# Cross attention: output projection and residual once per pair of batches

## The reference, cut

```python
x = x + attn(layernorm(x), ...)
x = x + xattn(layernorm(x), ctx_1024, ...)     # the part that is changed
x = x + ffn(layernorm(x), ...)

def xattn(query, value, wq, bq, wk, bk, wv, bv, wo, bo):   # 16 heads of 8
    q = split_heads(query @ wq.T + bq); k = split_heads(value @ wk.T + bk); v = split_heads(value @ wv.T + bv)
    attn = softmax(einsum('bhqd,bhkd->bhqk', q, k) / sqrt(8))
    ctx = einsum('bhqk,bhkd->bhqd', attn, v)
    return merge_heads(ctx) @ wo.T + bo
```

## Time and profile before

| what | before |
|---|---|
| median of 3 runs | 630.91 us (628.44 to 633.17) |
| the profiled execution | 632.53 us, its span 630.3 us |
| mean granted TensorE clock | 0.978 |
| PE / PEld / DVE / ACT / POOL busy | 584.3 / 465.9 / 460.3 / 380.1 / 215.7 us |
| instructions | 17326 |

### The profile page before, as it was taken

The page is one execution under the profiler, slowest core; times in us unless marked ns, Lnnn a source line. Parts: engine busy times, 40 slices in busy tenths (PEclk is TensorE's granted clock), DMA queues, the critical chain, the costliest instruction groups (busy, mean ns, idle before and its releaser), DMA issues.

```text
span 630.3 us, 17326 instructions
## 1 busy us (share of the span) xinstructions
PE 584.3 (93%) x6542; PEld 465.9 (74%) x6542; DVE 460.3 (73%) x850; ACT 380.1 (60%) x602; POOL 215.7 (34%) x185
## 2 busy tenths in 40 slices
PE   3699787798999999999999999999999989999997
PEld 1566464476778778778777787877888768999985
DVE  4865456866887887887887887887787467676676
ACT  2457455265665665665665665665656676667762
POOL 4575324722242242242232232232221224433430
PEclk9889899799999999999999999999999999999999
DMA  5000005499266366366366366367380101211000
GB/s 219 1 3 3 0 2 119 86 192 210 77 148 147 99 146 151 93 146 156 88 146 162 88 141 166 88 137 172 79 197 3 51 1 60 73 62 57 1 0 34
DMA packets 25286, 59.91 MB, mean 95 GB/s; under 512 B 14104, under 2 KB 14488, under 8 KB 25248
## 3 DMA queue, kind: packets, MB, share of 16 engines
q1 hardware_dynamic: 25248, 59.38, 39.5%
HBM read 20.49 MB, written 0.52 MB: 33 GB/s over the span
## 4 chain that ended last, share of the span: by engine, by line
PE 68%; SPq 7%; ACT 3%; issue 3%; DVE 2%; DMA 1%; ACTq 0%; DVEq 0%
PE PS L1739 12%; PE PS L1723 12%; PE PS L1699 11%; PE PS L1869 6%; PE PS L225 6%; PE PS L1871 6%; PE PS L1870 5%; PE PS L217 5%; SPq L1080 3%; SPq L1073 3%; PE PS L1755 3%; ACT k_full L246 1%; SPq L1088 1%; DMA q_stack<-neg_rows 1%; PE PS L1709 1%
## 5 line engine op out<-in xcount | busy, mean ns | idle before, releaser
L1427 DVE TENSOR_REDUCE chunk_max<-PS 128x1 f32<-128x500 f32 x336 | 214.3, 673 | 60.8 <-PE PS L1699 59.2
L1268 ACT ACTIVATE P<-PS 125x896 f32<-125x896 f32 x192 | 173.5, 914 | 122.0 <-PE PS L1723 121.1
L1699 PE MATMUL PS<-k_hi,q_block_hi 128*128 128x500 f32 x336 | 131.2, 439 | 6.3 <-ACT k_full L246 3.3
L1723 PE MATMUL PS<-q_stack,k_stack 97*125 97x224 f32 x768 | 122.7, 283 | 3.3 <-DMA q_stack<-neg_rows 2.0
L1723 PEld LDWEIGHTS PS<-q_stack,k_stack 97*125 97x125 f32 x768 | 107.0, 190 | 18.2 <-issue 8.0
L255 POOL TENSOR_TENSOR k_lo<-k_full,k_hi 128x500 fp32r<-128x500 f32 x48 | 61.2, 1278 | 103.6 <-ACT k_full L246 101.3
L1699 PEld LDWEIGHTS PS<-k_hi,q_block_hi 128*128 128x128 f32 x336 | 61.0, 193 | 36.8 <-ACT k_full L246 16.7
L1739 PE MATMUL PS<-P,values 125*32 125x112 f32 x3072 | 83.6, 260 | 0.5 <-ACT P L1268 0.5
L1739 PEld LDWEIGHTS PS<-P,values 125*32 125x32 f32 x3072 | 72.0, 110 | 13.9 <-issue 10.7
L1161 POOL TENSOR_TENSOR q_stack<-q_copies,consts 96x896 fp32r<-96x896 f32 x16 | 26.9, 1678 | 132.0 <-PE PS L1723 131.6
L1592 DVE TENSOR_TENSOR PS<-gated,PS 128x448 f32<-128x448 f32 x64 | 40.2, 628 | 30.5 <-PE PS L1871 28.6
(11 more groups left out here) (192 smaller groups left out, 892.8 us busy)
## 6 DMA issues: line engine op xcount, KB each, us to landing
k_stack<-k_hi SPq DMA_DIRECT2D x128, 187.5 KB, 4.5
ctxT<-ctx_in SPq DMA_DIRECT2D x16, 750.0 KB, 4.4
k_stack<-k_lo SPq DMA_DIRECT2D x64, 187.5 KB, 4.5
w_gate_up<-wgu_in SPq DMA_DIRECT2D x8, 512.0 KB, 3.6
w_down<-wd_in SPq DMA_DIRECT2D x8, 256.0 KB, 3.7
q_stack<-neg_rows SPq DMA_DIRECT2D x112, 0.5 KB
mats<-mats_in SPq DMA_DIRECT2D x1, 832.0 KB, 5.6
q_copies<-q_hi SPq DMA_DIRECT2D x8, 98.0 KB, 4.6
```

What stands on the lines that cost most here:

```text
L1268: nc.scalar.activation(P[:, t % RING, :].rearrange("p (a n) -> p a n", a=2), PS[0:KR, 2 * (t % 2):2 * (t % 2) + 2, 0:HALF], ACT.Exp).then_ ...
L1427: nc.vector.tensor_reduce(out=chunk_max[:, n // KC, n % KC:n % KC + 1], in_=PS[:, max_bank(b, n), 0:KW], axis=AX.X, op=ALU.max).then_inc(m ...
L1699: nc.tensor.matmul(PS[:, max_bank(b, n), 0:KW], q_block_hi[:, j, 128 * t:128 * t + 128], k_hi[:, j, KW * c:KW * c + KW], start=True, stop= ...
L1723: last = nc.tensor.matmul(PS[0:KR, 2 * (t % 2) + g // 2, o:o + GH * N], k_stack[:, j, g, KR * t:KR * t + KR], q_stack[0:SHIFT_ROW + 1, j, ...
```

## The change

The projection and the residual are no longer done for each batch in the period behind it. They are done for both batches of a pair in slot 8 of the even period that follows, and for the last pair at the end. For this `heads_out2` has four parts of 2 x 64 columns, each batch's heads in its half, with the columns 56 to 63 of each half cleared once by POOL. The reciprocals have a tile of their own, `heads_inverse`. A projection loads all 128 columns of a part, and the residual adds 128 partitions. The counts of the semaphores follow the pairs. Before it writes the first half of a pair, `scale_heads` waits for the projection of the pair before.

Apart from this, the six matrices of the first stage move from `mats` into `mats1`, a tile of the first stage's memory, which stage two's tiles take over later. So there are two transfers for the weights in place of one, and the waits are for 48.

```diff
-                    sp.dma_start(mats[:, :, :], mats_in).then_inc(weights_loaded, 16)
+                    sp.dma_start(mats1[:, :, :], mats_in[:, 0:S1_MATS, :]).then_inc(weights_loaded, 16)
+                    sp.dma_start(mats[:, :, :], mats_in[:, S1_MATS:, :]).then_inc(weights_loaded, 16)
...
-            heads_out2 = sb2("heads_out2", [128, 4 * N])
+            heads_inverse = sb2("heads_inverse", [128, 4 * N])
+            heads_out2 = sb2("heads_out2", [128, 4, 2, PITCH])
...
                     pool.wait_ge(ones_ready, 1)
+                    nc.gpsimd.memset(heads_out2[:, :, :, N:PITCH], 0.0).then_inc(pads_cleared, 1)
+                    pool.wait_ge(pads_cleared, 1)
                     layernorm_power(pool, 4, slice(1, PAIRS))
...
-                        nc.vector.reciprocal(heads_out2[:, half], DEN[:, half]).then_inc(den_inverted, 1)
-
-                    def scale_heads(b):
+                        nc.vector.reciprocal(heads_inverse[:, half], DEN[:, half]).then_inc(den_inverted, 1)
+
+                    def scale_heads(b, j, u):
                         dve.wait_ge(den_inverted, 2 * b + 2)
-                        nc.vector.tensor_tensor(heads_out2[:, :], heads_out2[:, :], heads_sum[:, :], ALU.mult
-                                                ).then_inc(o_scaled, 1)
-
-                    def residual(b, j, u):
-                        dve.wait_ge(out_done, b + 1)
-                        r = slice(PITCH * j, PITCH * j + N)
-                        nc.vector.tensor_tensor(X[r, bass.ds(u, 1), :], X[r, bass.ds(u, 1), :],
-                                                OUT2[r, :].unsqueeze(1), ALU.add).then_inc(x2_ready, 1)
+                        if j == 0 and later(b, 2):
+                            dve.wait_ge(out_done, u)
+                        if isinstance(b, int) and b < 2:
+                            dve.wait_ge(pads_cleared, 1)
+                        by_part = [t[:, :].rearrange("p (a n) -> p a n", n=N) for t in (heads_inverse, heads_sum)]
+                        nc.vector.tensor_tensor(heads_out2[:, :, j, 0:N], *by_part, ALU.mult).then_inc(o_scaled, 1)
+
+                    def residual(u):
+                        dve.wait_ge(out_done, u + 1)
+                        nc.vector.tensor_tensor(X[:, bass.ds(u, 1), :], X[:, bass.ds(u, 1), :],
+                                                OUT2.unsqueeze(1), ALU.add).then_inc(x2_ready, 1)
...
-                                if t == OUT_SLOT:
-                                    residual(b - 1, 1 - j, u if j == 1 else u - 1)
+                                if t == OUT_SLOT and j == 0:
+                                    residual(u - 1)
...
-                    def project_out(b, j):
-                        pe.wait_ge(o_scaled, b + 2)
-                        take_bank(BANK_OF["out", 0], (x2_ready, b + 1))
+                    def project_out(u):
+                        pe.wait_ge(o_scaled, 2 * u + 3)
+                        take_bank(BANK_OF["out", 0], (x2_ready, u + 1))
                         for n in range(4):
-                            last = nc.tensor.matmul(OUT2[PITCH * j:PITCH * j + N, :], heads_out2[:, N * n:N * n + N],
+                            last = nc.tensor.matmul(OUT2, heads_out2[:, n, :, :].rearrange("p e n -> p (e n)"),
                                                     MAT[f"wo{n}"], start=(n == 0), stop=(n == 3))
                         last.then_inc(out_done, 1)
...
-                                if t == OUT_SLOT:
-                                    project_out(b - 1, 1 - j)
+                                if t == OUT_SLOT and j == 0:
+                                    project_out(u - 1)
...
                     for k in range(1, IT):
                         gates(0, 0, k)
-                    project_out(B - 1, 1)
+                    project_out(PAIRS - 1)
```

More of the change, by code:

```diff
@@ L40 @@
 MATS = ["Wqk_t", "Wv_t", "Wo_t", "Wqk_c", "Wv_c", "Wo_c", "wq", "wk", "wv", "wo0", "wo1", "wo2", "wo3"]
+S1_MATS = 6
 ROWS = ["gamma1", "gamma2", "bv", "bo"]
@@ L95, in build @@
         X = sb("X", [128, PAIRS, D])
-        mats = sb("mats", [128, len(MATS), D])
+        mats = sb("mats", [128, len(MATS) - S1_MATS, D])
         rows = sb("rows", [128, len(ROWS), D])
@@ L100, in build @@
         consts = sb("consts", [128, consts_in.shape[1]])
-        MAT = {n: mats[:, k, :] for k, n in enumerate(MATS)}
+        MAT = {n: mats[:, k, :] for k, n in enumerate(MATS[S1_MATS:])}
         ROW = {n: rows[:, k, :] for k, n in enumerate(ROWS)}
@@ L281, in build @@
         with s1:
+            mats1 = sb1("mats1", [128, S1_MATS, D])
+            MAT.update({n: mats1[:, k, :] for k, n in enumerate(MATS[:S1_MATS])})
             Z = sb1("Z", [128, PAIRS, D])
@@ L582, in _ @@
                     shift(1, 1)
-                    dve.wait_ge(weights_loaded, 32)
+                    dve.wait_ge(weights_loaded, 48)
                     nc.vector.tensor_tensor(wo_scaled[:, 0, :], MAT["Wo_t"], ROW["gamma1"], ALU.mult
@@ L669, in _ @@
                     turn_tokens(0)
-                    pe.wait_ge(weights_loaded, 32)
+                    pe.wait_ge(weights_loaded, 48)
                     for c in range(2):
@@ L1049, in build @@
             x2_ready = sem("x2_ready")
+            pads_cleared = sem("pads_cleared")
             TURN_REST, PROJECT_REST = 8, 12
@@ L1566, in period @@
                                 if t == SCALE_SLOT:
-                                    scale_heads(b - 1)
-                                if t == OUT_SLOT:
-                                    residual(b - 1, 1 - j, u if j == 1 else u - 1)
+                                    scale_heads(b - 1, 1 - j, u if j == 1 else u - 1)
+                                if t == OUT_SLOT and j == 0:
+                                    residual(u - 1)
                             if exists(mb, B):
@@ L1573, in period @@
                             if isinstance(b, int) and b == B - 2 and t == OUT_SLOT:
-                                dve.wait_ge(x2_ready, B - 2)
+                                dve.wait_ge(x2_ready, PAIRS - 1)
                                 norm_stats(range(PAIRS - 1))
@@ L1584, in _ @@
                         invert(B - 1, a)
-                    scale_heads(B - 1)
-                    residual(B - 1, 1, PAIRS - 1)
+                    scale_heads(B - 1, 1, PAIRS - 1)
+                    residual(PAIRS - 1)
                     def multiply(e, j, k):
@@ L1597, in split_hidden @@
                                                 ALU.subtract).then_inc(hidden_split, 1)
-                    dve.wait_ge(x2_ready, B)
+                    dve.wait_ge(x2_ready, PAIRS)
                     norm_stats(range(PAIRS - 1, PAIRS))
```

## The result

The changed kernel takes 625.62 us (median of 12 runs), the kernel before 630.94 us in the same comparison. The ratio is 0.9907, with a 95% interval of 0.9882 to 0.9932: 5.9 us less, between 4.3 and 7.4; the two medians by themselves differ by 5.3 us. Forecast were 626.2 us and 4.7 us. In a second comparison the ratio was 0.990 (0.9855 to 0.9945). In the comparisons of the experiments, three runs of the kernel before and one of a variant took 814 to 1835 us, and the ratios leave them out (the medians count them).

The account below looks back on a forecast made before the run. PE was taken to bound the kernel, busy 23.21 of 23.45 us a period in stage two. Removed projections save 5.5 us, wide loads lose 0.8: 630.9 - 4.7 = 626.2 us, range 622.0 to 630.0.

Parts of the forecast that it names:

- the larger term: Stage two, eight of sixteen projections removed: 5.5 us saved, 4.7 in odd periods 1 to 13 and 0.76 in period 15.
- the smaller term: The eight remaining projections load 128 columns instead of 56: 0.1 us lost each, 0.8 us in all.
- What bounds the kernel: Stage two: PE bounds it, busy 23.21 of 23.45 us a period; a projection costs the path 1.02 us.
- The odd periods lose 0.67 and not 1.01 us each: Slot 8, periods 1 to 13: waits for DVE leave 0.67 of the projection's 1.01 us, 4.7 us for seven periods.
- The two waits forecast: Odd periods: the turn waits for DVE's read of the values, slot 9's first maximum for DVE's reduction of maximum 0; 0.05 us latency.
- The last period: Period 15: the tile's scores after the removed projection wait for slot 7's exponentials and load 0.76 us earlier.
- The wide loads: Eight remaining projections: only the first load, behind its wait, is in the open; 0.8 us lost, between 0 and 3.8.
- What costs nothing: Residual, product with gaps, new wait in `scale_heads`, POOL's clearing, extra DMA at the start, and tail: each taken as 0.
- the whole projection is saved: Rival: DVE is less close behind PE, so eight projections save 8.2 us in all, 622.7 us; chance 0.2.
- Wide loads in the open: Rival: the 128-column loads of eight projections are exposed, 3.8 us lost, gain 1.7 us, 629.2 us; chance 0.13.
- no shorter period: Rival: another engine's beat takes the gain back in stage two, time stays 630.9 us; chance 0.08.
- a slow product: Rival: DVE's `scale_heads` product doubles from 1.48 us through gaps in its output, delaying the maxima; 640.4 us; chance 0.04.

Follow-up runs that it names:

- the variant with the split alone: Kernel before with only the weights' transfer split and the first stage's six matrices in that stage's memory; ratio 0.9996 to the kernel before.
- the variant with halves: Changed kernel, but a pair's projection done as matmuls of 64 columns, one per batch half (16 records), still in the even period; 625.83 us, ratio 0.9897.
- the variant with sixteen wide projections: Kernel before with its sixteen projections, each loading 128 columns, plus the tile with gaps and split weights; 627.56 us, ratio 0.993.

## Why the prediction was right

The range held the time, and the forecast was 0.6 us off the median. Point by point, the mechanism of the larger term was right and the sign of the smaller one was wrong. That the total is so near is in part luck: the smaller term was wrong by 2.7 us, and the runs tell the gain only to within 1.6 us either way.

- **What bounds the kernel.** Right. PE's work taken out of the path came back as time, and PE is still busy for 22.46 of 22.81 us.
- **The odd periods lose 0.67 and not 1.01 us each.** The six from 3 to 13 became shorter by 0.60 to 0.73 us, 4.1 us together and 0.68 in the mean. Seven make the 4.67 us of the table beside 4.7 forecast, but period 1 counts for nothing there, since its wait for `q_stack` differs from profile to profile. The two waits forecast are in the trace at the places named, with the latency taken. The experiment with the banks shows that it was these waits: with other banks for the turn and the maxima, the next maximum's load comes 0.49 us sooner. It also shows what I didn't see, that the next wait for DVE stands right behind: only 0.18 us of it stay.
- **The last period.** Forecast 0.76 us. The tile's scores after the place of the projection load 0.92 us behind those before it (479.03 to 479.95), where it was 1.64 (486.06 to 487.70 in the earlier trace rows): 0.72 us less, and they wait for the exponentials as forecast. Of the whole stretch 0.6 us stay, as PE's wait for `q_stack` at its start takes 0.12 us back:

```profile
479.95 0.51 PEld L1734 LDWEIGHTS PS<-q_stack,k_stack 97*125 97x125 f32 x4 [0.41 <-ACT P L1276]
```

- **The wide loads: the term that failed.** I had put 0.1 us of loss on each of eight projections, 0.8 us. Measured against the variant with the split alone, the even periods and the tail gain 1.53 + 0.33 = 1.9 us, so the term was wrong by 2.7 us, more than the distance between the 4.7 us of the sum and the 6.3 us of the trace; period 1 and the last period took some back. (Against the kernel before it looks like 2.2 us, since period 2 gains 0.64 us there where the others gain 0.2; the rest of that is the wait of 0.33 us shown with the result.) What I had read as the price of a wait ("behind its wait" the first load is in the open) was the price of a load with 64 columns or fewer. The earlier trace rows held the hint: ahead of L1755's first load stand 0.23 us of idle time and ahead of the turn's 0.18, and the trace has no such gap ahead of L225's, with 125 columns, which start 0.01 us behind the start of the matmul before them:

```profile
353.50 0.39 PE L1699 MATMUL PS<-k_hi,q_block_hi 128*128 128x500 f32 x1
353.51 1.06 PEld L225 LDWEIGHTS PS<-mats,ctxT 128*125 128x125 f32 x8
```

I noticed that the loads of L225 are hidden, and took it as a bound on the loss; that the kernel before itself paid for its narrow loads I didn't ask. The loss of 3.8 us that the prediction works out from the Trainium skill ("TensorE: Matmul & The Clock Gate", section "LDWEIGHTS (loading the stationary operand)") didn't come: the loads of L1766 lie under matmuls. By the columns over 1.2 that this section gives, a load of 56 columns takes 47 ns and one of 128 takes 107; the traces have 129 ns and 192 (the median of L1766's loads), so the difference agrees and the lengths don't, and the measured ones hold here.
- **What costs nothing.** Right in each point. POOL clears the padding in 0.16 us and then still stands idle for 0.69 us, where it was 0.91. At the start `gate` is issued at 3.56 us, 0.48 later than in the earlier trace rows, and PE's load starts at 11.96, where it was 11.99. DVE's product, into the tile with gaps, has a median of 1478 ns where it had 1482:

```profile
L1466 DVE TENSOR_TENSOR heads_out<-heads_inverse,heads_sum x16: 391/1478/1485, 159.9 to 489.1; 128x224 f32<-128x224 f32 x16
```

- **The rivals.** That the whole projection is saved, 8.2 us, would need 1 us from each odd period, and none gained that; the span's 8.08 us are near it only by the waits in periods 1 and 2 and by the wide loads. Wide loads in the open, no shorter period, and a slow product all fell.
- **A row that I didn't use.** The prediction could have been read off the kernel before. Its period 0 has no projection, and shows slot 8 as it would become:

```profile
142.34 0.40 PE L1699 MATMUL PS<-k_hi,q_block_hi 128*128 128x500 f32 x1
...
142.94 0.30 PE L1709 MATMUL PS<-consts,max_turn 128*128 128x128 f32 x1 [0.20 <-DVE values L263]
...
144.46 1.50 PEld L1739 LDWEIGHTS PS<-P,values 125*32 125x32 f32 x64 [0.36 <-issue]
```

From maximum 0 to `weigh` 2.12 us, with the turn waiting for the same values, against 2.71 us in a period with the projection: 0.59 us, close to the 0.67 worked out.

## What to carry to other kernels

To price a removal, look at what stands right behind the removed work, bank by bank, and find an instance in the trace where that work is absent: the first or the last round of a pipeline often has one. Idle time of 0.2 us with no cause ahead of a weight load is a cost too, and a wider load can be the cheaper one. Where two matmuls with 64 loaded columns each use different halves of the array, as in the variant with halves, count them once. And one profile of each kernel doesn't say what the change gives: a variant without the change showed here that 1.2 us of the traces' difference came from elsewhere.

## What the runs showed of the hardware

- A weight load of 56 or 64 columns started only 0.32 to 0.33 us after the start of the matmul before it (a 128x500 one), with 0.23 to 0.24 us of idle time ahead, and the full-width load behind the group waited another 0.17 to 0.18 us. With 72, 96 or 128 columns the first load started at or within 0.01 us of the start of that matmul, without idle time. It makes 0.2 us for each group of narrow loads of the projection. The last projection, behind another group of full-width loads, has 0.31 us ahead of its first load with 56 or 64 columns and 0.01 with 128.
- The loads of `weigh`, 32 columns each, stand in the same gaps in both kernels: the first load of a group starts, in the median, 0.32 us behind the start of the full-width matmul before it, and the full-width load behind the group waits 0.17 us. They stand there three times a period, and the kernel before is idle for 10.7 us ahead of them without a releaser, more than the whole change gives. No run widened these loads, so what could be won there isn't shown.

```profile
L1739 PEld LDWEIGHTS PS<-P,values 125*32 125x32 f32 x3072 | 72.0, 110 | 13.9 <-issue 10.7 <-ACT P L1268 2.8
```

- An f32 load took 129 ns with 56 columns, 137 with 64, 143 with 72, 163 with 96, 188 with 125 and 191 to 192 with 128.
- Sixteen matmul records of 64 loaded columns, alternating between the halves of the array, took 1.02 us, as eight of 56 columns in one half did (1.01 us).
- In the profile of the variant with sixteen wide projections PE waited 2.11 us for `q_stack` at the start of the last period, and behind it the granted clock fell. Windows of that kernel, the granted clock is the third column from the right:

```profile
470.00:475.00 5.00, 2.89 (x35) 2.44 (x30) 2.27 (x13) 2.20 (x3) 1.73 (x2) 0.79 0.03 5
475.00:480.00 5.00, 5.00 (x73) 4.67 (x62) 0.36 (x1) 1.60 (x3) 0.00 (x0) 0.53 0.01 3
```

And of its timeline, four `weigh`:

```profile
474.42 3.22 PE L1746 MATMUL PS<-P,values 125*32 125x112 f32 x64
```

They took 3.22 us there instead of 1.74, near what 1.2 instead of 2.4 GHz would make of them. This was seen in one execution; the changed kernel waits 0.78 us at this place and keeps its clock.
